# The last attention layer and the clustered layer: layer norm, similarity and keep put one period later in the pipeline

## The reference

```python
def _L3_xattn_ref(text, features, Wq_w, Wq_b, Wk_w, Wk_b, fn_w, qn_w, kn_w):
    features_n = rmsnorm(features, fn_w)
    Q = rmsnorm(text @ Wq_w.T + Wq_b, qn_w)
    K = rmsnorm(features_n @ Wk_w.T + Wk_b, kn_w)
    attn = softmax(Q @ K.T / sqrt(512))
    return attn @ features_n
def _L3_ffn_ref(input, weight, bias, centroids, assignments):
    dots = softmax(x @ centroids.T / 0.1)          # 64 clusters
    hits = dots > 0.01
    query_sel = any(hits, axis=1)                  # one flag for each token
    cluster_sel = any(hits, axis=0)                # one flag for each cluster
    row_sel = cluster_sel[assignments]
    dense = x @ weight.T + bias
    return where(query_sel[:, None] & row_sel[None, :], dense, 0)
x = x + _L3_xattn_ref(_layernorm(x), ctx, ...)
x = x + _L3_ffn_ref(_layernorm(x), weight, bias, centroids, assignments)
```

## Time and profile before

| | us |
|---|---|
| median of the three runs | 1647.35 |
| the profiled execution | 1645.78 |
| its span | 1643.8 |
| PE busy in the span | 1520.8 (93%) |
| DVE busy | 1057.8 (64%) |
| ACT busy | 820.7 (50%) |
| POOL busy | 348.1 (21%) |
| the last pipeline's first product (q_proj of tile 0) | starts at 1520.98 |
| the count of the hits | starts at 1633.38 |

### The profile page before, as it was taken

The page is one execution under the profiler, slowest core; times in us unless marked ns, Lnnn a source line. Parts: engine busy times, 40 slices in busy tenths (PEclk is TensorE's granted clock), DMA queues, the critical chain, the costliest instruction groups (busy, mean ns, idle before and its releaser), DMA issues.

```text
span 1643.8 us, 27777 instructions
## 1 busy us (share of the span) xinstructions
PE 1520.8 (93%) x9626; PEld 1328.7 (81%) x9626; DVE 1057.8 (64%) x2559; ACT 820.7 (50%) x2866; POOL 348.1 (21%) x364
## 2 busy tenths in 40 slices
PE   6999999999999998889999999999999988767895
PEld 5899999999999987778888888888888776655684
DVE  6566556655665678756666666666666878756563
ACT  4455545545545563345555555565555515633541
POOL 4102011110101022222222222231322213421320
PEclk9999999999999999999999999999999999879996
DMA  5101010100001001011010100010101011110101
GB/s 189 44 27 33 33 30 33 55 27 27 26 27 39 27 25 52 17 48 39 27 39 27 40 26 40 27 39 27 53 12 34 21 39 33 36 58 1 33 4 52
DMA packets 14192, 60.22 MB, mean 37 GB/s; under 512 B 2036, under 2 KB 3444, under 8 KB 8936
## 3 DMA queue, kind: packets, MB, share of 16 engines
q1 hardware_dynamic: 14056, 58.46, 10.1%
HBM read 56.36 MB, written 2.10 MB: 36 GB/s over the span
## 4 chain that ended last, share of the span: by engine, by line
PE 51%; issue 28%; DVE 12%; ACT 4%; POOL 4%; DMA 0%; DVEq 0%; POOLq 0%; ACTq 0%; SPq 0%
PE psY L808 12%; PE psQ L733 8%; PE psKV L753 7%; PE psSO L796 2%; PE psSO L702 2%; PE psQ L718 2%; PE psKV L1096 2%; PE psQ L1058 1%; PE psTP L718 1%; POOL wo L460 1%; PE psSO L703 1%; PE psTP L763 1%; PE psTP L781 1%; DVE hT L1563 1%; DVE wq L1563 1%
## 5 line engine op out<-in xcount | busy, mean ns | idle before, releaser
L808 PE MATMUL psY<-wo,oT 128*128 128x512 f32 x1536 | 384.7, 399 | 1.8 <-DVE oT L1563 1.3
L808 PEld LDWEIGHTS psY<-wo,oT 128*128 128x128 f32 x1536 | 278.6, 188 | 65.7 <-POOL wo L460 2.2
L733 PE MATMUL psQ<-wq,hT 128*128 128x512 f32 x768 | 211.2, 413 | 1.6 <-DVE wq L1563 1.6
L460 POOL TENSOR_TENSOR wo<-stage_o,wo 128x512 fp32r<-128x512 f32 (+2 forms) x75 | 96.8, 1316 | 341.0 <-ACT wo L1152 334.0
L561 POOL TENSOR_TENSOR rms<-ms_eps,minus_half 128x5 f32<-128x5 f32 x64 | 74.7, 1167 | 392.5 <-DVE ms_eps L1726 392.5
L733 PEld LDWEIGHTS psQ<-wq,hT 128*128 128x128 f32 x768 | 136.9, 192 | 25.7 <-DVE wq L1563 2.4
L1221 ACT ACTIVATE prob<-s_sb,neg_mx 128x64 f32<-128x64 f32 x256 | 86.1, 337 | 110.5 <-DVE neg_mx L1713 110.5
L1224 ACT ACTIVATE prob<-wide,neg_mx 128x128 f32<-128x128 f32 x256 | 99.8, 391 | 74.3 <-DVE neg_mx L1713 74.1
L1152 ACT ACTIVATE pT<-psTP 128x512 fp32r<-128x512 f32 (+1 forms) x128 | 62.3, 486 | 131.3 <-PE psTP L781 131.3
L753 PEld LDWEIGHTS psKV<-wkv,arena 128*128 128x128 f32 x768 | 100.7, 192 | 19.9 <-DVE kT L1563 15.6
L753 PE MATMUL psKV<-wkv,arena 128*128 128x256 f32 x768 | 105.0, 287 | 9.2 <-DVE kT L1563 9.2
(11 more groups left out here) (275 smaller groups left out, 3249.8 us busy)
## 6 DMA issues: line engine op xcount, KB each, us to landing
stage_q<-in_wq SPq DMA_DIRECT2D x16, 1024.0 KB, 5.4
stage_o<-in_wo SPq DMA_DIRECT2D x16, 1024.0 KB, 4.8
stage_kv<-in_wkv SPq DMA_DIRECT2D x12, 512.0 KB, 3.6
stage_q<-in_ctx SPq DMA_DIRECT2D x16, 256.0 KB, 2.9
stage_o<-in_ctxT SPq DMA_DIRECT2D x2, 1024.0 KB, 7.5
stage_q<-in_base SPq DMA_DIRECT2D x2, 1024.0 KB, 5.6
out<-x_res SPq DMA_DIRECT2D x8, 256.0 KB, 2.3
x_res<-in_x SPq DMA_DIRECT2D x1, 1536.0 KB, 14.2
```

The source lines that it names most:

```text
L460: g.tensor_tensor(dst[LO], stage, dst[HI].bitcast(f32), ALU.subtract).then_inc(ld[what + "_lo"], 1)
L733: m = mm(psQ[:], lat(xl, k, n), wq[:, wl, k, :], start=k == 0 and i == 0, stop=k == KT - 1 and i == 2)
L808: m = mm(psY[:], oT[:, ol, h, :], wo[:, wl, h, :], start=h == 0 and i == 0, stop=h == HQ - 1 and i == 2)
```

## The change

It renumbers the periods and moves calls within the loop bodies of PE, ACT, DVE and POOL; no instruction is added or taken away, and none changes its shape. On PE `ln_transpose` of tile c goes from the middle of period c + 3 to its end, and `similarity` of a tile from its period n + 3 to n + 4. `dense` of tile n stays in period n + 4: at the end for tiles 0 to 3, in the place of `q_proj` for tiles 4 to 6 (as before for 4 and 5), at the end for tile 7. On DVE `x_add` and `ln_stats` of a tile go from the end of period n + 2 into the first half of period n + 3, `ln_lo` and `hit_max` into period n + 4, `hits_of` into n + 5; `keep` stays in period n + 5 but goes from its first place to one behind `normalise`. On ACT `ln_hi` goes to the head of the next period and `ln_norm_act` behind `f_hi`. On POOL `ln_rstd` and `nmr` go to the head of the period. `features` and `q_scale` change places.

```diff
--- before.py
+++ after.py
@@ -619,19 +619,18 @@
             g.tensor_tensor(f_r[:, n % 3, LO], stage_q[:, n % 4], f_r[:, n % 3, HI].bitcast(f32),
                             ALU.subtract).then_inc(N3["f_lo"], 1)
 
-        for p in range(NT + 2):
-            a, b = p - 1, p - 2
-            if 0 <= a < NT:
-                power("q", a, 0)
-                f_lo(a)
+        for p in range(NT + 3):
+            if 0 <= p - 3 < NT:
+                ln_rstd(7, p - 3)
+                pool.wait_ge(LNS[7]["rstd"], ln_at(7, p - 2))
+                pool.wait_ge(LNS[6]["xn"], ln_at(6, NT))
+                g.tensor_scalar(nmr[:, p - 3:p - 2], mv[:, p - 3, 0:1], rstd[:, p - 3:p - 2], -1.0, ALU.mult,
+                                ALU.mult).then_inc(M["nmr7"], 1)
+            if 0 <= p - 1 < NT:
+                power("q", p - 1, 0)
+                f_lo(p - 1)
             if p < KT:
                 low("wo", halves(wo, p), stage_o[:, p], 71 + p + 1)
-            if 0 <= b < NT:
-                ln_rstd(7, b)
-                pool.wait_ge(LNS[7]["rstd"], ln_at(7, b + 1))
-                pool.wait_ge(LNS[6]["xn"], ln_at(6, NT))
-                g.tensor_scalar(nmr[:, b:b + 1], mv[:, b, 0:1], rstd[:, b:b + 1], -1.0, ALU.mult,
-                                ALU.mult).then_inc(M["nmr7"], 1)
 
 
     @block.tensor
@@ -1096,29 +1095,26 @@
                         mm(psKV[:], lat(xl, k, n), wo[:, wl, k, :], start=k == 0 and i == 0, stop=False)
                 add_bias(psKV[:], "o").then_inc(C3["dense"], 1)
 
-            for p in range(NT + 3):
+            for p in range(NT + 4):
                 a, b, c, d = p - 1, p - 2, p - 3, p - 4
                 if 0 <= b < NT:
                     scores(b)
                 if 0 <= a < NT:
                     q_transpose(a)
-                if p == NT + 2:
+                if p < NT:
+                    q_proj(p)
+                elif d < NT - 1:
+                    dense(d)
+                if 0 <= b < NT:
+                    p_transpose(b)
+                if 0 <= d < NT:
+                    similarity(d)
+                if 0 <= b < NT:
+                    attend(b)
+                if 0 <= d and (p < NT or d == NT - 1):
                     dense(d)
                 if 0 <= c < NT:
                     ln_transpose(next_ln, c, lambda: need(pe, LNS[next_ln]["lo"], ln_at(next_ln, c)))
-                if p < NT:
-                    q_proj(p)
-                elif p < NT + 2:
-                    dense(d)
-                if 0 <= b < NT:
-                    p_transpose(b)
-                if 0 <= c < NT:
-                    similarity(c)
-                if 0 <= b < NT:
-                    attend(b)
-                if 0 <= d and p < NT:
-                    dense(d)
-            dense(NT - 1)
 
         def clustered():
             s = C3
@@ -1516,24 +1512,24 @@
                                      scale=1.0 / TEMPERATURE, accum_out=small[:, 14:15]).then_inc(C3["exp"], 1)
 
             act.wait_ge(s["k"], NT)
-            for p in range(NT + 3):
-                a, b, c = p - 1, p - 2, p - 3
-                if 0 <= c < NT:
-                    ln_norm_act(7, c)
+            for p in range(NT + 4):
+                a, b, c, d = p - 1, p - 2, p - 3, p - 4
+                if 0 <= d < NT:
+                    ln_hi(next_ln, d)
                 if 0 <= a < NT:
                     qT_hi(a)
                 if 0 <= b < NT:
                     exps(b)
-                if 0 <= c < NT:
-                    ln_hi(next_ln, c)
                 if 0 <= a < NT:
                     f_hi(a)
+                if 0 <= c < NT:
+                    ln_norm_act(7, c)
                 if 0 <= b < NT:
                     pT_hi(b)
                 if p < NT:
                     q_read(p)
-                if 0 <= c < NT:
-                    hit_exps(c)
+                if 0 <= d < NT:
+                    hit_exps(d)
                 if p < KT:
                     high("wo", wo[:, HI, p], stage_o[:, p], 21 * 16)
 
@@ -2058,37 +2054,37 @@
                 V.scalar_tensor_tensor(kept(n), psKV[:], q_any[:, n:n + 1], x[:, n], ALU.mult,
                                        ALU.add).then_inc(C3["kept"], 1)
 
-            for p in range(NT + 3):
-                a, b, c, d = p - 1, p - 2, p - 3, p - 4
-                if 0 <= d - 1 < NT - 1:
-                    keep(d - 1)
+            for p in range(NT + 5):
+                a, b, c, d, e = p - 1, p - 2, p - 3, p - 4, p - 5
+                if 0 <= d < NT:
+                    ln_lo(next_ln, d)
+                if 0 <= c < NT:
+                    x_add(c)
                 if 0 <= b < NT:
                     row_max(b)
+                if 0 <= e < NT:
+                    hits_of(e)
+                if 0 <= c < NT:
+                    dve.wait_ge(s["x_add"], c + 1)
+                    ln_stats(next_ln, c)
                 if 0 <= a < NT:
                     mean_square("q", a, 8, 0)
                     qT_lo(a)
                 if 0 <= b < NT:
                     normalise(b)
-                if 0 <= c < NT:
-                    ln_lo(next_ln, c)
+                if 0 <= e < NT - 1:
+                    keep(e)
+                if p < NT:
+                    features(p)
                 if 0 <= a < NT:
                     q_scale(a)
-                if p < NT:
-                    features(p)
                 if 0 <= b < NT:
                     pT_lo(b)
-                if 0 <= c < NT:
-                    hit_max(c)
-                if 0 <= b < NT:
-                    x_add(b)
-                    dve.wait_ge(s["x_add"], b + 1)
-                    ln_stats(next_ln, b)
                 if p == NT + 2:
-                    keep(d)
-                if 0 <= c < NT:
-                    hits_of(c)
-            dve.wait_ge(ld["asg_in"], 16)
-            V.tensor_scalar(prob[0:64], q_sb[0:64].bitcast(i32), row_id[0:64], None, ALU.is_equal)
+                    dve.wait_ge(ld["asg_in"], 16)
+                    V.tensor_scalar(prob[0:64], q_sb[0:64].bitcast(i32), row_id[0:64], None, ALU.is_equal)
+                if 0 <= d < NT:
+                    hit_max(d)
 
         def clustered():
             s = C3
```

## The result

| | before | after |
|---|---|---|
| median of the runs, us | 1646.57 (4 runs, 1644.76 to 1647.93) | 1663.15 (4 runs, 1662.93 to 1670.31) |
| profiled execution, its span | 1645.78, 1643.8 | 1670.56, 1668.7 |
| stage, from its first q_proj to the count of hits | 1520.98 to 1633.38 = 112.40 | 1529.16 to 1657.98 = 128.82 |

The medians differ by 16.6 us, where 8.0 were forecast, and the result is outside the range. The ratio of the means is 1.0112, interval 1.0083 to 1.0141; the run of 1670.31 is in it. The profiled execution of after lost 8.2 us ahead of the stage (1529.16 for 1520.98), where both kernels do the same work. Much of that is the clock: in the windows from 1300 to 1400 the mean granted clock is 0.95 before and 0.86 after, and 0.09 of 100 us is 9 us (an estimate).

The account below looks back on a forecast made before the run. PE bounds the middle; the last 40 us are bound by the path PE, ACT, DVE, PE and the clock. Warm-up gains 6.1 us, periods 5 to 7 lose 5.2, the tail 8.9: 1647.35 + 8.0 = 1655.4, range 1649.5 to 1660.5.

Parts of the forecast that it names:

- Warm-up: First q_proj to period 5: PE's idle wait ahead of the norm transpose goes, so period 5 starts 6.1 us earlier.
- Closed loop: Periods 5 to 7: DVE's chain starts at PE's period end and PE waits for it; 12.75 us a period, not 11.02.
- Rival 4: Periods 5 to 7 stay at 11.02 us because DVE keeps pace; 5.2 us less, 1650.2; chance 0.07.
- rival 1: Periods 5 to 7: features starts before POOL's f_lo and lasts 0.75 us; period 11.9, total 1652.9; chance 0.14.
- Periods 5 to 7: Step costing PE's waits of 0.5 and 1.2 us a period, 5.2 us over three periods, with denses at full clock.
- rival 3: TensorE's clock falls in periods 5 to 7 too, each dense costing 1.9 to 2.5 us more; 1662; chance 0.07.
- Tail: Periods 8 to 11: three denses wait for DVE's late keep, gaps of 4.6, 4.4 and 4.7 us; 8.9 us more.
- Rival 2: TensorE's clock holds at the end, for three denses and the last similarity and dense; 8.6 us less, 1646.8; chance 0.12.

Follow-up runs that it names:

- e3: Changed kernel plus PE products whose result nobody reads, in the gaps of periods 5 to 7 and ahead of the denses of tiles 4 to 6; 1649.17 us.
- e1: Changed kernel with DVE's hits_of and keep of the tile before moved to the head of each period; 1635.89 us.
- e4: Changed kernel with features moved behind q_scale and pT_lo on DVE; 1657.08 us.
- g9: e4 plus two products whose result nobody reads, ahead of the softmax's transpose in periods 5 to 7; 1653.06 us.
- f6: Kernel before the change plus PE products whose result nobody reads, ahead of six of its waits; 1637.49 us.

## Why the prediction was wrong

The direction held, and so did the places and lengths of the waits. The size was off by 8.4 us of stage, and all but some 0.4 of it is one term, TensorE's clock. By the prediction's own parts, each with its excess over the forecast:

| part | forecast | measured | excess |
|---|---|---|---|
| warm-up, first q_proj to period 5 | 33.42 | 33.49 | 0.07 |
| periods 5 to 7 | 3 x 12.75 = 38.25 | 14.44 + 14.15 + 15.54 = 44.13 | 5.88 |
| periods 8 to 11 | 48.75 | 15.07 + 14.09 + 12.42 + 9.62 = 51.20 | 2.45 |

- **Warm-up**, right. The gap ahead of attend was 0.76, 0.85 forecast, and period 4 took 11.00 (1551.65 to 1562.65). Before it was 39.49, so 6.0 gained.
- **Closed loop**, right. The gaps are 0.64 and 0.99 for 0.5 and 1.2, features takes 1.62 behind f_lo. With the clock held, in e3, a period is 12.86: the loop's own price is 0.1 a period over the forecast. Rival 4 (DVE keeps the pace) is out, and so is rival 1: f_lo came 0.20 us first. e1 shows what breaks the loop, the keep and the hits out of the chain, and then the period is 10.97.
- **The failed step: "Periods 5 to 7", which costed the loop's waits as idle time alone.** That was rival 3's question, and I gave it 0.07. The runs showed that the products behind the waits fell to 1.2 GHz in each of the three periods (denses of 4.05, 3.58 and 4.95 for 2.9), which cost 44.13 - 38.58 (e3's three periods) = 5.6 us. That is 1.9 us a period, at the lower end of rival 3's 1.9 to 2.5 a dense. That its total of 1662 is near the 1663.15 measured is partly luck, since 2.45 us of the excess were lost in the tail. What I held against it was that transposes ran at full pace behind the second gap of 2.00 in the earlier trace rows. That row shows a gap that did not cost, and the row above it an equal one that did (1.12 us). One of each is no ground for 0.07. The q_proj that follows in each case says the same: 3.92 us behind the first gap and 3.01 behind the second. e4 has the same: of gaps of 0.64, 0.68 and 0.64 the first left the dense at 2.88 and the other two did not. Six gaps in three periods need only one or two to fall badly. Near half would have been fair, by my judgement; no run gives a chance.
- **Tail**, waits right: the three denses start 6.54, 5.88 and 4.76 us into their periods, 6.5, 5.8 and 4.7 forecast. The term mis-sized is the dense behind a wait. I took 4.79 from one row, behind a wait of 3.41; behind 4.34 to 4.54 it is 5.31 to 5.46, at a clock of 0.50 to 0.52. With what follows up to the next stage's start that is 5.97, 5.67 and 5.94 for 5.15 each, 2.1 of the 2.45; the earlier trace rows had a 5.37 that would have served. The prediction names three waits at the end of the kernel before and leaves out a fourth, ahead of that very dense:

```profile
1605.20 1.12 PE L650 MATMUL psTP<-ident,xn 128*128 128x128 f32 x4 [2.46 <-ACT xn L1415]
```

  So the longer dense stood behind the shorter wait, 5.37 behind 2.46 and 4.79 behind 3.41, and the length of a wait doesn't give the dense's time. The last dense adds 0.4 (5.08 for 4.71), and its similarity came in 0.2 below the forecast.
- **Rival 2** (the clock holds at the end) fell: denses of 5.4 for the 2.9 it needed. e3 shows its price for them was rightly worked out, since with fillers the three denses take 2.9 to 3.0.

What stays open is why one gap of 0.64 to 0.68 lowers the clock and the next doesn't; one of 0.76 in the changed kernel (at 1550.48) left the next period at 11.00. It would take the same period at many offsets, which was not tried.

## What to carry to other kernels

Cost a gap on TensorE twice: as idle time, and as a chance that the products behind it run at half clock. A gap of 0.64 to 0.68 us once a period cost 1.6 us more in two periods of three here (e4 against g9), so look for each new gap, even one under 1 us, in a stretch that had none. Where DVE's period is a chain that PE waits for in the middle, put at its head what needs only last period's results (keep and hits: 25 us of stage between the changed kernel and e1). A wait that can't be removed can be filled with products whose result nobody reads and that depend only on what is there already (1637.49 for 1645.01 in f6). Fillers that outlast the wait cost time of their own: in e3 those ahead of dense(6) held it up by 1.3 us.

## What the runs showed of the hardware

- Idle times under 1 us can be enough to drop TensorE to its lower level: with e4's gaps filled (g9), the clock stayed at 1.00. In the changed kernel the clock by windows of 1 us is 1.00 until the gap of 0.99, then 0.50, and 1.00 again from 1575:

```profile
1570.00:1571.00 1.00, 0.04 (x1) 0.00 (x0) 0.97 (x4) 0.43 (x2) 0.04 (x1) 1.00 0.00 0
1571.00:1572.00 1.00, 0.97 (x3) 0.78 (x4) 0.26 (x2) 0.41 (x2) 0.00 (x0) 0.65 0.00 0
1572.00:1573.00 1.00, 1.00 (x4) 0.81 (x3) 0.00 (x0) 0.00 (x0) 0.00 (x0) 0.50 0.00 0
1573.00:1574.00 1.00, 1.00 (x4) 0.71 (x4) 0.00 (x0) 0.00 (x0) 0.00 (x0) 0.50 0.07 16
1574.00:1575.00 1.00, 1.00 (x4) 0.83 (x3) 0.00 (x0) 0.00 (x0) 0.00 (x0) 0.64 0.00 0
1575.00:1576.00 1.00, 1.00 (x6) 0.75 (x4) 0.00 (x0) 0.00 (x0) 0.00 (x0) 1.00 0.00 0
```

  The values between 0.50 and 1.00 stand in the two windows where the level changes. PE was busy from the end of the gap at 1571.03 all through the slow windows. The Trainium skill ("TensorE: Matmul & The Clock Gate", section "A second HAM failure mode: psum-queue depth-cycling") tells of a kernel whose brief pauses between groups of products make the clock go back and forth; this trace agrees, 0.88 over a period with PE busy for 12.81 of 14.44 us.
- Fillers keep it up although what PE waits for comes no sooner: 0.73 us of them a period raised a clock of 0.87 over two periods to 1.00 (g9 against e4), 43 products in six places brought denses of 4.35 to 5.37 us to 3.00 (f6 against the earlier trace rows).
- A DVE instruction with two inputs in SBUF took 0.75 us when it began ahead of POOL's, and 1.62 when POOL's had begun 0.20 us before, ending 0.55 us after it. POOL's took 1.27 us when it began first and 1.42 when DVE's had begun 0.46 us before.
